# Recurrent attention block on one core: where the gate's expansion and half of k's projection stand in TensorE's program

## What is computed

```python
q, k, v = silu(x @ Wq), silu(x @ Wk), silu(x @ Wv)
log_f = log_sigmoid(x @ Wf1 @ Wf2);  beta = sigmoid(x @ Wbeta) * 2
k = k / sqrt(sum(k*k) + eps)                       # per head
# two steps per token: decay with a correction, then the token's own k, v
S = exp(g)*S + a[..., None]*(b @ S) + k[..., None]*v
o = q @ S                                          # read after the second step
y = o * sigmoid(x @ Wog1 @ Wog2)                   # the gate
y = y / sqrt(mean(y*y) + eps) * norm_w
x = layernorm(x + y @ Wo)
x = layernorm(x + x @ W.T + b + x @ lilora.T)      # feed-forward with a merged low-rank weight
```

## Time and profile before

| | us |
|---|---|
| median of 3 runs | 2545.72 |
| lowest and highest | 2537.54, 2548.74 |
| profiled execution, device time | 2542.35 |
| its span, first to last instruction | 2540.3 |
| TensorE busy in it | 2217.9 (87%) |
| VectorE, ScalarE busy | 1602.5, 1617.1 (63%, 64%) |
| GpSimd busy | 458.9 (18%) |
| mean granted TensorE clock | 0.962 |

### The profile page before, as it was taken

The page is one execution under the profiler, slowest core; times in us unless marked ns, Lnnn a source line. Parts: engine busy times, 40 slices in busy tenths (PEclk is TensorE's granted clock), DMA queues, the critical chain, the costliest instruction groups (busy, mean ns, idle before and its releaser), DMA issues.

```text
span 2540.3 us, 225123 instructions
## 1 busy us (share of the span) xinstructions
PE 2217.9 (87%) x102472; PEld 1698.5 (67%) x102472; DVE 1602.5 (63%) x3940; ACT 1617.1 (64%) x3048; POOL 458.9 (18%) x555
## 2 busy tenths in 40 slices
PE   5788899998999999999999999999999999898784
PEld 2566666776676777667667666777776667676673
DVE  2566466776666676666677766666776666776533
ACT  3556466666666666666666666666666676666543
POOL 1011112212121221122122112211121211212110
PEclk8889899999999999999999999999999999999886
DMA  3244355544555543455545445554444555544431
GB/s 99 77 125 116 111 153 153 145 122 127 144 150 153 152 141 113 130 151 153 153 142 147 118 130 150 145 154 142 133 122 145 146 150 153 144 136 120 138 119 40
DMA packets 693526, 338.99 MB, mean 133 GB/s; under 512 B 552354, under 2 KB 652320, under 8 KB 693408
## 3 DMA queue, kind: packets, MB, share of 16 engines
q1 hardware_dynamic: 693408, 337.76, 46.3%
HBM read 35.66 MB, written 16.78 MB: 21 GB/s over the span
## 4 chain that ended last, share of the span: by engine, by line
PE 86%; issue 10%; DVE 2%; ACT 1%; DMA 0%; SPq 0%; ACTq 0%; DVEq 0%
PE bank L583 15%; PE bank L746 13%; PE bank L725 11%; PE bank L717 8%; PE bank L737 7%; PE bank L729 5%; PE bank L606 5%; PE bank L635 5%; PE bank L696 5%; PE bank L656 3%; PE bank L707 3%; PE bank L615 2%; PE bank L600 2%; PE bank L590 2%; PE bank L597 1%
## 5 line engine op out<-in xcount | busy, mean ns | idle before, releaser
L479 POOL TENSOR_TENSOR state<-moved,edge 128x512 f32<-128x512 f32 x252 | 292.3, 1160 | 1739.5 <-DVE moved L1108 1739.5
L725 PE MATMUL bank<-parts,w_now 32*32 32x64 f32 x16512 | 417.7, 222 | 4.6 <-DMA w_now<-w_row 3.2
L583 PE MATMUL bank<-x_col,w_kqv 128*128 128x512 f32 x768 | 372.0, 621 | 48.5 <-issue 47.7
L729 PE MATMUL bank<-aq_now,delta 32*32 32x16 f32 x16512 | 401.5, 179 | 7.7 <-issue 7.7
L871 ACT ACTIVATE parts<-bank,cf 128x256 f32<-128x256 f32 x512 | 214.8, 471 | 295.0 <-DVE o_col L1102 285.3
L729 PEld LDWEIGHTS bank<-aq_now,delta 32*32 32x32 f32 x16512 | 389.4, 109 | 8.3 <-issue 8.3
L725 PEld LDWEIGHTS bank<-parts,w_now 32*32 32x32 f32 x16512 | 375.8, 110 | 16.6 <-issue 4.9
L746 PE MATMUL bank<-uq_now,s_now 32*32 32x24 f32 x32768 | 360.7, 188 | 12.4 <-issue 12.4
L746 PEld LDWEIGHTS bank<-uq_now,s_now 32*32 32x32 f32 x32768 | 335.7, 106 | 18.6 <-issue 12.9
L1102 DVE TENSOR_TENSOR o_col<-qs,bank 128x64 f32<-128x64 f32 x512 | 89.4, 215 | 359.7 <-PE bank L729 358.6
L1131 DVE COPY_PREDICATED aq<-ci,bank 128x128 f32<-128x128 int32 x256 | 77.2, 301 | 355.5 <-PE bank L717 224.0
(11 more groups left out here) (99 smaller groups left out, 3753.9 us busy)
## 6 DMA issues: line engine op xcount, KB each, us to landing
s_now<-state SPq DMA_DIRECT2D x256, 256.0 KB
uq_now<-uqv SPq DMA_DIRECT2D x256, 192.0 KB, 2.4
t_now<-t_t SPq DMA_DIRECT2D x256, 128.0 KB
w_now<-w_row SPq DMA_DIRECT2D x256, 128.0 KB
uq_a<-uqv SPq DMA_DIRECT2D x64, 384.0 KB, 3.1
low<-uqv SPq DMA_DIRECT2D x64, 384.0 KB
x_col<-in_xt_dram SPq DMA_DIRECT2D x32, 512.0 KB, 4.8
w_a<-w_col SPq DMA_DIRECT2D x64, 256.0 KB, 3.8
```

The source lines that it names most:

```text
L479: pool.tensor_tensor(state[:, qc, :, :, :].rearrange("p m b v -> p (m b) v"), moved[m % 2][:, :, :, :].rearrange("p m b v -> p (m b) v"), ...
L583: mm = pe.matmul(ps[:, :], w_kqv[:, a, w, f * P:(f + 1) * P], x_col[:, a, :], start=a == 0, stop=a == KT - 1)
L725: pe.matmul(ds_bank[quarter(h), m, :, :].rearrange("p b v -> p (b v)"), w_now[quarter(h), m, :], parts[quarter(h), m, :, :].rearrange("p b ...
L729: mm = pe.matmul(o_bank[quarter(h), m, :], delta[quarter(h), m, :], aq_now[quarter(h), m, :], start=True, stop=True)
```

## The change

Two new tables of TensorE's work, `dense0_last` and `dense1_last`, are called after the second scores of slots 0 and 1. The gate's expansion moves from the head of slot 1 to the end of slot 0. The first half of k's projection moves from the head of slot 2 to the end of slot 1. Slot 1's scores then follow `right_sides()` with nothing between. The order in `FILLS`, the banks and the programs of all the other engines stay as they are. Each of slots 0 and 1 has one more two-way branch.

```diff
--- before.py
+++ after.py
@@ -644,9 +644,12 @@
                 if there(j + 1):
                     project(j, "v", 2, 1)
 
-            def dense1(j):
+            def dense0_last(j):
                 if there(j + 1):
                     expand_gate(j)
+
+            def dense1(j):
+                pass
 
             def dense1_more(j):
                 if there(j + 2):
@@ -656,10 +659,13 @@
                         mm = pe.matmul(ps[:, :], w_small[:, a, :], x_col[:, a, :], start=a == 0, stop=a == KT - 1)
                     mm.then_inc(filled["small"].handle, 1)
 
+            def dense1_last(j):
+                if there(j + 2):
+                    project(j, "k", 0, 0)
+
             def dense2(j):
                 if there(j + 2):
-                    for f in range(HF):
-                        project(j, "k", 0, f)
+                    project(j, "k", 0, 1)
                 if there(j + 1):
                     turn_scores(j)
 
@@ -709,6 +715,7 @@
 
             dense = (dense0, dense1, dense2, dense3, dense4, dense5, dense6, dense7)
             more = (dense0_more, dense1_more)
+            final = (dense0_last, dense1_last)
 
             def scores(c):
 
@@ -799,6 +806,7 @@
                         pair(0)
                         some(0, 2, more)
                         pair(1)
+                        some(0, 2, final)
                     with pe.Else():
                         some(2, 4)
                 with pe.Else():
@@ -825,6 +833,7 @@
                         first_pair(j, 2 * n)
                         more[n](j)
                         first_pair(j, 2 * n + 1)
+                        final[n](j)
                     if j == -2 and 2 <= n < 5:
                         merge(n - 2)
             pe.wait_ge(lora_copied.handle, 2 + KT)
@@ -854,6 +863,7 @@
                 updates()
                 dense[n](G)
                 more[n](G)
+                final[n](G)
             for n in range(2, CH):
                 dense[n](G)
             for n in range(CH):
```

## The result

The changed kernel takes 2567.86 us (median of four runs, 2565.85 to 2570.65), the kernel before 2541.87 us over four. The ratio is 1.0116, with a 95% interval of 1.0092 to 1.0140: slower by 26 us as the medians have it and by 29 us as the ratio has it, where +22.5 and a time of 2567 were forecast. The profiled execution's span went from 2540.3 to 2564.0 us.

A forecast was written before the change was run, and what follows sets the result against it. TensorE's own instruction stream, with late starts behind small matmuls, was taken as the bound. 28 groups at +0.84 us, +1.1 for group 30 and -2.1 for groups 0 and 1 gave +22.5, put at 2567 us; range 2548 to 2588.

The forecast's parts named there:

- The mechanism: End of slot 0: gate's second expansion (L590) waits for ScalarE's silu of v0, 0.8 to 0.9 us some 29 times.
- (a): End of slot 0, T being the second scores' end: gate's second expansion waits for silu of v, +2.20, -0.10 us.
- (b): Head of slot 1: gate leaves, -1.17 us; longer gap before scores, +0.15; later small projection, +0.10.
- the prediction's rule: TensorE's queue holds 64 instructions, so scores use up any lead; the small projection's gap would stay at 0.26 us.
- (c): End of slot 1: late start of 0.69 us goes, half of k's projection comes, its bank costs no wait; +1.37 us.
- (d): Slot 2: one half of k's projection remains before the transposes instead of two; -1.71 us.
- The sum: Per group, from slot 0's second scores to slot 2's first transpose, all terms together: +0.84 us.
- The start of the program: Groups 0 and 1, where v's silu is early and no wait arises: -1.06 us each, 2.1 us less.
- The clean end: End of slot 0: v's bank free when the gate wants it, both gaps gone, -1.06 us per group, 2513; chance 0.08.
- Late starts in other places: Gaps return at slot 1's scores, small projection, k and behind the wait: +1.77 us a group, 2594; chance 0.12.

The follow-up runs named there:

- e1: The changed kernel with the gate's expansion back at the head of slot 1, so only half of k's projection moves; ratio to the kernel before 0.9977.
- e2: The changed kernel with both halves of k's projection back in slot 2, so only the gate's expansion moves; ratio to the kernel before 1.0278.
- e4: e3 with VectorE also taking both norms' statistics ahead of the first mask of the scores; ratio to the kernel before 0.9921.
- e9: The kernel before with only the new ScalarE and VectorE order of e4, TensorE's order being the old one; ratio to the kernel before 1.0034.
- e10: The changed kernel with one more activation, about 0.4 us, on ScalarE ahead of silu of v0; ratio to the kernel before 1.0387.
- e3: The changed kernel with ScalarE's normalising of the feed-forward's rows moved behind silu of v and the scores' second copy; ratio to the kernel before 1.0201.
- e11: The kernel before with the added two-way branch, empty both ways, at the end of slots 0 and 1; ratio to the kernel before 1.0010.
- e5: The kernel before with slot 1 reordered to scores, gate's expansion, scores, small projection; ratio to the kernel before 0.9987.
- e6: e2 with the gate's first expansion issued twice into the same bank, giving TensorE work during the wait; ratio to the kernel before 1.0204.
- e8: e4 with the old ScalarE and VectorE order kept in the last three iterations, which have no scores left; 2508.9 us, ratio to the kernel before 0.9887.
- e7: The changed kernel with the gate's first expansion issued twice into the same bank; ratio to the kernel before 1.0098.

## Why the prediction was right

**The mechanism** held: L590 waits for silu of v0 29 times (0.73 us each, where 0.8 to 0.9 was said), e1, e2, e4 and e9 put the loss on that one wait, and e10 shows that it has no slack: 0.39 us later at silu is 0.38 us more in the group.

**(a)** The wait was forecast to end at T + 1.86 and `deltas()` to start at T + 2.86. They came at T + 1.79 (1251.02 - 1249.23) and T + 2.84. Two small errors cancel: a bank freed by ScalarE took 0.04 us to reach TensorE here, not the 0.14 of the earlier trace rows, and an expansion alone takes 1.12 us, not 1.0.

**(b)** is the term that was too small. The gap before the scores grew by 0.10 (0.63 after 0.53), and I had taken 0.15. But `right_sides()` ahead of it is now recorded at 1.41 us, where the kernel before has 1.26 in that slot (it started at 1244.56 and slot 1's gate at 1246.35, 1.79 later; now it is 2.05 to the scores). So the head of slot 1 cost +0.26 (medians of the groups at full clock: +0.31, of which 0.11 is the gap and 0.20 `right_sides()`). In e3 and e4 `right_sides()` takes 1.26 us at that place behind the same `deltas()` without a gap. So the 0.15 to 0.20 us come neither from the gap that went nor from the wait alone; they go with ScalarE's old order, and the way they come about stays open. The prediction had no term for them. The small projection's gap is 0.28 after 0.26. That it stays is what the prediction's rule from the Trainium skill's TensorE: Matmul & The Clock Gate (Part 1, on queue depths) would have, and I had given it +0.10; still its start came 0.12 us later behind the start of the scores, since the scores took 1.69 us and not 1.58. **(c)** came out as forecast: 0.16 and 1.91. So did **(d)**: 1.82.

**The sum** was +0.84 a group and is +0.95 (20.67 - 19.72), or +0.92 in the group shown.

**Outside the sum** several things that I did not price nearly cancel. The five groups with a low clock in slot 1 cost 9.9 us; the kernel before loses 8.0 in seven groups in the middle of its program, and the changed kernel does not. The start of the program, to the third group, is 6.9 us shorter, where I had 2.1: the kernel before has a late start of 5.0 us at the first pass of the loop, the one long one of the earlier trace rows, which the changed kernel lacks. That this is the reason isn't shown: e1_k_only keeps it (4.9 us) and its start of the program is 6.7 us shorter all the same, and e9 and e11, with TensorE's work in the old order, are 3.0 and 2.3 us shorter there. One profile of each can't tell such a shift from chance. The stretch behind the loop is 3.1 us longer. 27.5 - 6.9 + 3.1 = 23.7 us of span. So the total was met with a per-group sum that was a tenth too small, with a shorter start that I can't explain, and by luck in the clock: e2 and e3, with much the same wait, lost 37 to 44 us to it, which the range to 2588 did not allow for.

**The rivals.** The clean end was a matter of the other engines' order: given a free bank (e4) it is worth 0.81 us a group against the kernel before. I had put it at 1.06, but with the 0.80 us gap of an early group, where a group of the loop has 0.66; with that it is 0.92. Late starts in other places did appear, 0.04 to 0.15 us at each (e5, e11), never the 0.3 us behind the wait: `deltas()` follows the second expansion at once.

## What to carry to other kernels

Dense work at the end of a loop's body hides the loop's own branches and waits, but only if that work can start; before moving it forward, follow its bank back to the engine that frees it, through every way that leads there, and compare the time at which the bank comes free with the time at which the moved work would start. Where the bank is late, move the work that frees it (here two reorderings on engines with slack turned a loss of 1.2% into a gain of 1.1%). And price an idle moment on TensorE at more than its length: in this kernel it could bring the clock down for several microseconds after.

## What was unexpected of the hardware

- **A wait of 0.7 to 1.1 us can halve the granted clock behind it.** It is 0.50 for 3.4 to 10.2 us, costing 0.9 to 3.3 us a time: in 5 of 26 groups of the changed kernel, 14 in e3, 19 in e2, 22 in e10 with 0.38 us more of wait. With the same work and no wait (e4) there is none in that slot.
- **The clock also falls in the midst of unbroken 32x32 matmuls** (2.70 of 2.70 us busy before it in e6), and in slots 3 to 7 of the kernel before seven times, about 1.1 us each. What decides which groups it meets stays open: kernels that differ by 0.4 us in a group differ by 14 such groups.
- **ScalarE's order changes the time of small matmuls that wait for nothing in the profile.** `right_sides()` of slot 1 takes 1.26 us in the kernel before, e3, e4 and e8, and 1.40 to 1.49 us in the changed kernel, e2, e6, e7 and e10. Between the changed kernel and e3 only ScalarE's program differs. The cause stays open.
